# Softplus of the scan's step sizes: tanh inside the loop over time, one Ln table behind it, clips on GpSimd

## The reference, cut to what matters

```python
xz = jnp.einsum('bld,ed->ble', x, W_in)           # x after a layer norm
xc, z = (xz[..., :d_inner], xz[..., d_inner:])
conv = ... + conv_b                               # causal, 4 taps, per channel
u = jax.nn.silu(jnp.swapaxes(conv, 1, 2))
x_dbl = jnp.einsum('bld,ed->ble', u, W_x)
dt_raw, Bp, Cp = x_dbl[..., :1], x_dbl[..., 1:17], x_dbl[..., 17:]
dt = jnp.clip(jax.nn.softplus(dt_raw * W_dt + b_dt), 0.0001, 10.0)
A = -jnp.exp(jnp.minimum(A_log, 5.0))
# for every time step: h = clip(h * exp(clip(dt*A)) + clip(dt*B*u)), y = sum_n h*C
```

## Time and profile before

| | us |
|---|---|
| median of three executions | 1990.7 |
| the profiled execution | 1989.05 |
| its span, first to last instruction | 1987.2 |
| PE, DVE, ACT, POOL busy in it | 1602.9, 1403.6, 989.3, 484.3 |
| loop of `scan_inputs`, first transpose to last Abs | 1051.3 to 1171.0 |
| tail of softplus to the first instruction of `scan_states` | 1171.0 to 1197.0 |
| `scan_states` | 1197 to 1568 |

### The profile page before, as it was taken

How to read it: one execution, slowest core, us unless ns; L and a number is a source line. 1 busy time by engine, 2 the same in 40 slices (tenths; PEclk the granted TensorE clock), 3 DMA queues, 4 the chain that set the end, 5 groups by cost and what they waited for, 6 DMA issues and landing times. The chain is left out here.

```text
span 1987.2 us, 37884 instructions
## 1 busy us (share of the span) xinstructions
PE 1602.9 (81%) x11056; PEld 1044.5 (53%) x11056; DVE 1403.6 (71%) x3795; ACT 989.3 (50%) x2687; POOL 484.3 (24%) x503
## 2 busy tenths in 40 slices
PE   6999999999998997888967845776776433698998
PEld 3666666666664554555645744565665433243443
DVE  5777777777775665666864447999999855576775
ACT  3666666666663332333322258999999410111110
POOL 1111111111111010000001107888888551000000
PEclk9999999999999998998988977889888766799999
DMA  4111011110109100001660000000000000000000
GB/s 128 33 32 30 23 32 32 32 32 21 32 12 292 47 0 1 1 0 54 195 202 0 0 0 0 1 0 1 1 0 0 11 0 21 28 6 11 6 6 16
DMA packets 69349, 66.54 MB, mean 33 GB/s; under 512 B 5695, under 2 KB 66834, under 8 KB 69266
## 3 DMA queue, kind: packets, MB, share of 16 engines
q1 hardware_dynamic: 66598, 64.00, 10.7%
q10 hardware_dynamic: 2668, 1.62, 0.3%
HBM read 61.41 MB, written 4.19 MB: 33 GB/s over the span
## 5 line engine op out<-in xcount | busy, mean ns | idle before, releaser
L1962 PE MATMUL ss_y_ps<-ss_h,ss_diag 128*128 128x256 f32 x1024 | 266.1, 424 | 132.1 <-ACT sc_dt L1880 92.0
L1962 PEld LDWEIGHTS ss_y_ps<-ss_h,ss_diag 128*128 128x128 f32 x1024 | 217.2, 215 | 180.7 <-issue 93.9
L595 ACT ACTIVATE x_probs<-x_probs,x_neg_max 128x257 f32<-128x257 f32 x512 | 253.6, 498 | 63.2 <-DVE x_neg_max L696 63.2
L696 DVE CUSTOM_DVE_ANT_0 x_probs<-x_s_ps,x_mask_b 128x257 f32<-128x257 f32 x512 | 187.2, 422 | 132.6 <-PE x_s_ps L403 132.6
L1864 ACT ACTIVATE ss_decay<-sc_dt,sc_a 128x256 f32 (+1 forms) x496 | 207.1, 473 | 1.8 <-DVE ss_h L1927 1.8
L1918 DVE SCALAR_TENSOR_TENSOR ss_decay<-ss_decay,ss_h 128x1024 f32<-128x1024 f32 x124 | 152.3, 1228 | 29.3 <-ACT ss_decay L1864 29.1
L1874 ACT ACTIVATE ss_come<-ss_dtu,sc_xd 128x256 f32<-128x256 f32 x384 | 163.1, 507 | 6.6 <-POOL ss_dtu L1820 6.6
L1834 POOL TENSOR_TENSOR ss_diag<-all_ident,sc_xd 128x512 f32<-128x512 f32 x128 | 160.7, 1256 | 11.4 <-PE ss_y_ps L1962 1.4
L413 PE MATMUL x_pT_ps<-all_ident,x_probs 128*128 128x128 f32 x1024 | 162.0, 281 | 0.6 <-DVE x_pT L703 0.6
L703 DVE COPY x_pT<-x_pT_ps 128x512 f32<-128x512 f32 x256 | 161.2, 668 | 0.0
L1927 DVE CUSTOM_DVE_ANT_0 ss_h<-ss_come,ss_decay 128x1024 f32<-128x1024 f32 x124 | 149.9, 1209 | 0.0
(11 more groups left out here) (363 smaller groups left out, 3110.2 us busy)
## 6 DMA issues: line engine op xcount, KB each, us to landing
x_ctx_t<-ctxT SPq DMA_DIRECT2D x48, 514.0 KB, 3.8
kept_ctx_t<-ctxT SPq DMA_DIRECT2D x16, 514.0 KB, 7.9
kept_ctx_n<-ctx SPq DMA_DIRECT2D x16, 512.0 KB, 8.4
x_ctx_n<-ctx SPq DMA_DIRECT2D x16, 512.0 KB, 4.0
all_x<-x SPq DMA_DIRECT2D x4, 512.0 KB, 7.3
x_mid<-all_x SPq DMA_DIRECT2D x32, 64.0 KB, 3.8
all_x<-x_mid SPq DMA_DIRECT2D x4, 512.0 KB, 7.5
out<-all_x SPq DMA_DIRECT2D x8, 256.0 KB, 2.0
```

Source lines behind the costliest of these rows:

```text
L595: ins = nc.scalar.activation(probs[p][:, n, :], probs[p][:, n, :], ACT.Exp, scale=-1.0, bias=neg_max[p][:, n:n + 1], accum_out=sums[p][:, ...
L696: vec.tensor_tensor_reduce(probs[p][:, n, :], s_ps[:, c, 0:S2], mask_b[:, :], -1.0, -MASKED, ALU.add, ALU.min, neg_max[p][:, n:n + 1]).the ...
L1962: ins = nc.tensor.matmul(y_ps[p][:, 0:DI], diag[q][:, m, :], h[q][:, m, :], start=(q == 0 and m == 0), stop=(q == NQ - 1 and m == NH - 1))
```

## The change

The Tanh of half the absolute value is taken per time step within the loop, three steps behind, on ACT. The tail then has only four Ln on ACT, with a scale of 0.5 and a bias of 0.5 from a new tile `half` that one more DVE memset fills. Exp of `a` moves behind the Ln. DVE subtracts the Ln instead of adding it, and the four clips move from DVE to POOL, where each waits for the DVE instruction before it.

```diff
+        half = sb("half", [P, 1])
-            pe.wait_ge(prep, TAPS + 2 + 9)
+            pe.wait_ge(prep, TAPS + 3 + 9)
...
                     nc.scalar.activation(soft[:, t - 2, :], dt[:, t - 2, :], ACT.Abs).then_inc(abs_sb, 1)
+                if inside(t - 3):
+                    act.wait_ge(abs_sb, t - 2)
+                    act.sem_inc(waited, 1)
+                    nc.scalar.activation(soft[:, t - 3, :], soft[:, t - 3, :], ACT.Tanh, scale=0.5).then_inc(tanh_sb, 1)
...
-            pipeline(act, step, 2, 2, TAPS)
-
-            act.wait_ge(abs_sb, T)
+            pipeline(act, step, 2, 3, TAPS)
+
+            for q in range(LN_Q):
+                t = slice(q * LT, (q + 1) * LT)
+                act.wait_ge(tanh_sb, (q + 1) * LT)
+                nc.scalar.activation(soft[:, t, :], soft[:, t, :], ACT.Ln, scale=0.5, bias=half[:, :]).then_inc(ln_sb, 1)
             act.wait_ge(a_step, 1)
             nc.scalar.activation(a[:, :], a[:, :], ACT.Exp).then_inc(a_step, 1)
-            for half in range(2):
-                quarters = range(half * LN_Q // 2, (half + 1) * LN_Q // 2)
-                for q in quarters:
-                    s = slice(q * LT, (q + 1) * LT)
-                    nc.scalar.activation(soft[:, s, :], soft[:, s, :], ACT.Exp, scale=-1.0).then_inc(exp_sb, 1)
-                for q in quarters:
-                    s = slice(q * LT, (q + 1) * LT)
-                    act.wait_ge(exp_sb, q + 1)
-                    nc.scalar.activation(soft[:, s, :], soft[:, s, :], ACT.Ln, bias=1.0).then_inc(ln_sb, 1)
...
             pool.wait_ge(uz_sb, T)
+            for q in range(LN_Q):
+                s = slice(q * LT, (q + 1) * LT)
+                pool.wait_ge(soft_sb, q + 1)
+                pool.sem_inc(waited_pool, 1)
+                nc.gpsimd.tensor_scalar(dt[:, s, :], dt[:, s, :], 1e-4, 10.0, ALU.max, ALU.min).then_inc(clip_sb, 1)
...
+            vec.memset(half[:, :], 0.5).then_inc(prep, 1)
...
                 dve.wait_ge(ln_sb, q + 1)
-                vec.scalar_tensor_tensor(dt[:, s, :], dt[:, s, :], 0.0, soft[:, s, :], ALU.max, ALU.add).then_inc(soft_sb, 1)
-                dve.wait_ge(soft_sb, q + 1)
-                vec.tensor_scalar(dt[:, s, :], dt[:, s, :], 1e-4, 10.0, ALU.max, ALU.min).then_inc(clip_sb, 1)
+                vec.scalar_tensor_tensor(dt[:, s, :], dt[:, s, :], 0.0, soft[:, s, :], ALU.max, ALU.subtract).then_inc(soft_sb, 1)
```

More of the change, by code:

```diff
@@ L1636, in scan_inputs @@
         waited_pool = sem("waited_pool")
-        waited, abs_sb, exp_sb, ln_sb, soft_sb, clip_sb = (sem(n) for n in ("waited", "abs_sb", "exp_sb", "ln_sb", "soft_sb", "clip_sb"))
+        waited, abs_sb, tanh_sb, ln_sb, soft_sb, clip_sb = (sem(n) for n in ("waited", "abs_sb", "tanh_sb", "ln_sb", "soft_sb", "clip_sb"))
         block = ctx.enter_context(nc.Block())
@@ L1762, in _ @@
             vec.tensor_scalar(a[:, :], a[:, :], 5.0, None, ALU.min).then_inc(a_step, 1)
-            dve.wait_ge(prep, 2)
-            split_row(vec, dve, prep, TAPS + 2, cb3[:, :], rowmask, (c_hi[:, :], c_rest[:, :], c_f[:, :]), cb[0:3, :])
+            dve.wait_ge(prep, 3)
+            split_row(vec, dve, prep, TAPS + 3, cb3[:, :], rowmask, (c_hi[:, :], c_rest[:, :], c_f[:, :]), cb[0:3, :])
             pipeline(dve, step, 3, 1, TAPS)
```

## The result

The changed kernel took 2001.29 us (median of four, 1999.58 to 2002.31) against 1989.82 us before (four, 1987.5 to 1991.46). The ratio is 1.0058, with a 95% interval of 1.004 to 1.0075: 0.6% slower, where 0.3% faster was forecast. The profiled execution took 2002.31 us, its span 2000.5 us.

The account below looks back on a forecast made before the run. Stages run serially: PE paces the loop, a serial ACT-DVE chain the tail, ACT the scan. Gains of 5.4 (tail) and 0.25 (load), 5.7 us together, take 1990.7 to 1985.0 us; range 1981.0 to 1988.0.

Parts of the forecast that it names:

- Clips on POOL: Tail: each 128x2048 clip takes 1.90 us on POOL, and subtractions and clips block each other, 16.0 us in all.
- the gain of 5.4 in the tail: Tail: the last clip ends at 1190.98, so POOL opens the scan at 1191.5 instead of 1196.95, 5.4 us earlier.
- the 0.25: Start of the scan: gain in us from the table load no longer needed ahead of the first decays.
- Rival C: Tail: POOL clips at the pace of two-input instructions, c (a clip's length) 4.7 us; 5.5 us slower, 1996.2 us; 3%.
- Rival D: Loop: Tanh not hidden or needing table loads around it each step; 10 us slower in all, 2001 us; 1%.
- Tanh in the loop: Loop on ACT: 32 Tanh of 0.42 us hide in the Silu's 2.5 us wait for PE, cost 0.
- the further 1.4 us: ACT's tail: a drain of some 1380 ns the Trainium skill adds to a table load; weighed and not counted.
- The memset: Preparation on DVE: one more memset delays PE's start by 0.14 us at most, taken as 0.1.
- The alternation of POOL and DVE: Tail: each engine waits for the other's whole instruction, so four subtractions and four clips take 16.0 us.
- The load ahead of the decays: Start of the scan: a 1.28 us table load on ACT goes, but waiting for `dtu` leaves a gain of 0.25 us.
- the formula 8.4 + 4c: Tail: time in us from first subtraction to last clip, c being a clip's length; 16.0 with c at 1.90.
- Rival A: Tail: POOL and DVE do not block each other; tail ends at S (first subtraction's start) + 10.8, gain 10.9, 1979.8 us; 8%.

Follow-up runs that it names:

- swap_min_max: The changed kernel with the POOL clip's operations exchanged, min with 10 first, then max with 1e-4: 1979.96 us against 1988.04 for the kernel before, ratio 0.9963.
- scan_bound_swapped: The kernel before with only the POOL bound in the scan (line 1829) turned from min-max to max-min: 2260.87 us, one run, 271 us slower.
- clip_in_loop: The changed kernel without clips in the tail, v clipped instead in the loop on DVE: 1976.14 us against 1989.45 for the kernel before, ratio 0.9931.
- pool_clips_alone: The kernel before with only the four clips moved to POOL, as max-min: 2003.9 us against 1989.45, ratio 1.0071.

## Why the prediction was wrong, point by point

**The step that failed** is the price of a clip in "Clips on POOL": "Such a clip on 128x1024 takes 1.04, ... by that slope it is 1.90, at most twice 1.04 = 2.08". The row is of min-max and the change writes max-min, and no row of before shows max-min, or any other such pair, on POOL. The "at most" was no bound at all. With 7.07 for 1.90 the gain of 5.4 in the tail becomes a loss of 12.9. With the fast pair in its place the rest of the prediction's tail holds: in `swap_min_max` it gains 5.5 us (20.9 against 26.4). The total there is 8.1 us below the kernel before, where 5.7 was forecast; what goes beyond the tail and the 0.25 has no cause shown by any run. Rival C put the loss at the right place, a dearer clip, but took its size, c = 4.7, from POOL's two-input instructions; it was given 3% and dismissed with "line 1829 is the same instruction with two constants, in place". `scan_bound_swapped` shows that it was not the same. Rival D names 2001 us, the time that was measured, but this is chance: the loop is no longer, and no table load stands in it behind the Silu's first one.

**Right, by rows of after:**
- Tanh in the loop costs nothing: ACT waits 2.21 for PE instead of 2.51, the loop is no longer.
- The load starts 1.05 behind the start of the last Abs (1.08 forecast), the first Ln 1.29 behind the load: there is no room for the further 1.4 us that the prediction weighed and turned down. The first subtraction comes 4.37 behind the last Abs, where 1174.98 - 1170.57 = 4.41 was forecast; the 4.41 holds 0.1 for the memset, which lies ahead of the loop, and the first Ln, 1.99 instead of 1.90, happens to make up for it.
- The memset was put at 0.1 and cost 0.08: from the memset of `ones` to PE's first instruction it is 5.66 (1047.15 to 1052.81), before 5.58 (1045.79 to 1051.37).
- 0.53 from the last clip to `dtu`.
- The alternation of POOL and DVE: 16.0 us in `swap_min_max`, to the tenth and in its order, and with it that the move costs time even with the fast pair (20.9 against 18.8 in the tail). The Trainium skill's rule (SBUF — State Buffer, Summary: rules for kernel authors), that a DVE instruction with two SBUF inputs and a GpSimd one that reads SBUF block each other until the first is through, is borne out by the records of 3.98 us there; with the slow clips it holds only in part, as the next paragraph shows.
- The load ahead of the decays: 0.25 forecast, 0.15 measured (first `dtu` to the start of the last pair on line 1930, 364.75 against 364.90), with ACT waiting 1.22 for `dtu`.

**Half right:** for slow clips the formula 8.4 + 4c gives 36.7; measured are 34.4 from the first subtraction to the last clip. The rows of the changed kernel in which the two engines meet:

```profile
1178.67 8.87 POOL L1738 TENSOR_SCALAR sc_dt<-sc_dt 128x2048 f32<-128x2048 f32 x1 [9.25 <-DVE sc_dt L1774]
1180.52 6.58 DVE L1774 SCALAR_TENSOR_TENSOR sc_dt<-sc_dt,si_soft 128x2048 f32<-128x2048 f32 x1
1187.62 8.61 POOL L1738 TENSOR_SCALAR sc_dt<-sc_dt 128x2048 f32<-128x2048 f32 x1
1189.22 7.03 DVE L1776 TENSOR_SCALAR sc_a<-sc_a 128x16 f32<-128x16 f32 x1
```

The third subtraction (start 1180.52, length 6.58) ended at 1187.10, 0.44 before the clip for which it should have waited (1178.67 + 8.87 = 1187.54), and that clip was no longer for it (6.9 us from the end of the second subtraction at 1180.61). With 2.14 of work (its 2.29 less the 0.15 of start-up that the prediction reads from rows 6) DVE was busy with it during the slow clip's last 2.6 us, an estimate, and one subtraction less stands between the clips. Rival A (no blocking at all) is wrong: in `swap_min_max` it would give 10.8.

## What to carry to other kernels

Price an instruction on GpSimd only from a row with the same operations in the same order: swapping the two halves of a clip, which changes no result when the bounds are ordered, was worth 5.2 us in each of four clips here (18.4 us of the tail, 39.3 against 20.9) and 271 us in the scan. A monotonic function lets a clip be moved ahead of it, into a loop with room; here that took 5.0 us off the serial tail (13.8 against 18.8 with the clips on DVE) and cost 0.9 in the loop. And an upper bound taken from a row that differs in anything from the new instruction is an estimate, not a bound.

## What the runs showed of the hardware that was not expected

- POOL's tensor_scalar on 128x2048 in fp32, SBUF in place, with immediate constants: min-max and mult-add 1.89 us, max-min and min-min 7.07, one operation alone 5.36. A single operation is 2.8 times as long as a fast pair. The single operations, min-min and mult-add rest on one run each.
- DVE shows no such difference: its max-min takes 1.23 on 128x2048 and 0.29 on 128x256 (`clip_in_loop`), its min-max 0.69 on 128x1024 (line 1951 in the changed kernel), all near one straight line (0.53 ns for each further element).
- A slow POOL instruction let a DVE subtraction run in its last 2.6 us, as above (in `pool_clips_alone` too one ended 0.44 ahead of its clip); the fast ones of `swap_min_max` did not. The scan of `scan_bound_swapped` shows the same: DVE's product of two SBUF tiles took 1.93 us instead of 1.23, its median in the kernel before, and ended 1.5 us ahead of the slow bound, by the same reckoning in its last 2.6 us.

```profile
1234.74 3.62 POOL L1829 TENSOR_SCALAR ss_come<-ss_come 128x1024 f32<-128x1024 f32 x1
1234.92 1.93 DVE L1909 TENSOR_TENSOR ss_come<-ss_dtu,sc_xd 128x1024 f32<-128x1024 f32 x1 [5.20 <-POOL ss_dtu L1820]
```

- But DVE's small multiply of 128x16, issued at 1189.22 in the changed kernel, was held for 7.03 us, to the end of the second clip (1187.62 + 8.61 = 1196.23). When a slow one blocks and when not stays open; it was not tried by itself.
- Ln with its bias from a tile takes 1.986 us, with the bias 1.0 of before 1.901; the first of the four is on the path, the other three are off it.
